# Four recurrent layers on one core: two sets of semaphores in turn, cleared by the next stage

## What is computed

```python
xn = _layernorm(x); s = _L0_attn_ref(xn, ...); g = _silu(_L0_ffn_ref(xn, ...)); x = x + s * g
xn = _layernorm(x); s = _L1_attn_ref(xn, ...); g = _silu(_L1_ffn_ref(xn, ...)); x = x + s * g
xn = _layernorm(x); s = _L2_attn_ref(xn, ...); g = _silu(_L2_ffn_ref(xn, ...)); x = x + s * g
xn = _layernorm(x); s = _L3_attn_ref(xn, ...); g = _silu(_L3_ffn_ref(xn, ...)); x = x + s * g
```

## Time and profile before

| | |
|---|---|
| three runs | 4060.0, 4065.36, 4072.39 us; median 4065.36 |
| the profiled execution: its time | 4061.12 us |
| its span in the trace | 4059.4 us |
| its mean granted TensorE clock | 0.967 of full speed |
| busy over the span | PE 85%, DVE 63%, ACT 44%, POOL 24% |
| DMA engines, mean over the span | 34 GB/s |

### The profile page before, as it was taken

The page is one execution under the profiler, slowest core; times in us unless marked ns, Lnnn a source line. Parts: engine busy times, 40 slices in busy tenths (PEclk is TensorE's granted clock), DMA queues, the critical chain, the costliest instruction groups (busy, mean ns, idle before and its releaser), DMA issues. The chain is left out here.

```text
span 4059.4 us, 56138 instructions
## 1 busy us (share of the span) xinstructions
PE 3448.3 (85%) x19803; PEld 1796.0 (44%) x19959; DVE 2564.1 (63%) x5512; ACT 1772.8 (44%) x3776; POOL 971.1 (24%) x809
## 2 busy tenths in 40 slices
PE   4888888888988889888988889888898888888877
PEld 2344434444344443444444443454434444444444
DVE  4566665666566665676556665666656766566665
ACT  1544434443444435444344444444354443444424
POOL 1032311332023320233113320233202231133234
PEclk7999999999999999999999999999999999999988
DMA  5000011101001020000110010110200101000130
GB/s 159 31 13 27 30 39 32 30 9 63 5 32 37 1 67 22 22 27 30 39 32 23 16 59 9 32 37 1 67 14 23 33 27 41 32 15 23 52 94 22
DMA packets 86675, 138.68 MB, mean 34 GB/s; under 512 B 12270, under 2 KB 61240, under 8 KB 83960
## 3 DMA queue, kind: packets, MB, share of 16 engines
q1 hardware_dynamic: 79636, 124.11, 9.6%
q10 hardware_dynamic: 6756, 10.87, 0.9%
HBM read 105.06 MB, written 29.10 MB: 33 GB/s over the span
## 5 line engine op out<-in xcount | busy, mean ns | idle before, releaser
L633 DVE TENSOR_REDUCE nmax<-banks 128x1 f32<-128x512 f32 (+3 forms) x1216 | 760.6, 658 | 415.5 <-PE banks L446 223.5
L556 ACT ACTIVATE probs<-banks 128x512 f32<-128x512 f32 (+3 forms) x1024 | 475.2, 526 | 291.6 <-PE banks L465 203.6
L446 PE MATMUL banks<-ks,qs 72*128 72x512 bf16 (+3 forms) x1536 | 442.4, 333 | 100.3 <-DVE nmax L633 60.5
L465 PE MATMUL banks<-qs,ks 74*128 74x512 bf16 (+3 forms) x1536 | 445.5, 331 | 47.7 <-ACT probs L556 19.7
L97 PE MATMUL banks<-filler,identb 128*128 128x512 bf16 x1632 | 425.0, 389 | 27.1 <-PEq L77 19.6
L446 PEld LDWEIGHTS banks<-ks,qs 72*128 72x128 bf16 x1536 | 141.4, 98 | 385.5 <-DVE nmax L633 214.8
L97 PEld LDWEIGHTS banks<-filler,identb 128*128 128x128 bf16 x1776 | 172.6, 100 | 222.8 <-issue 79.6
L556 ACT ACTIVATE early<-banks 128x256 f32<-128x256 f32 (+3 forms) x512 | 194.7, 440 | 169.7 <-PE banks L465 167.7
L1493 ACT ACTIVATE probs<-banks,nm 128x192 f32<-128x192 f32 x512 | 172.6, 422 | 214.0 <-DVE nm L1445 214.0
L515 PE MATMUL banks<-probs,v 128*32 128x512 f32 (+3 forms) x2048 | 234.4, 529 | 21.7 <-DVE att L620 10.3
L1527 POOL TENSOR_TENSOR probs<-probs,inv 128x768 f32<-128x768 f32 x128 | 187.2, 1467 | 253.8 <-DVE inv L1455 253.8
(11 more groups left out here) (490 smaller groups left out, 6661.9 us busy)
## 6 DMA issues: line engine op xcount, KB each, us to landing
qs<-parts_scratch SPq DMA_DIRECT2D x300, 96.0 KB
ks<-parts_scratch SPq DMA_DIRECT2D x288, 96.0 KB
parts_scratch<-parts SPq DMA_DIRECT2D x50, 384.0 KB, 2.5
shared<-in_w_h SPq DMA_DIRECT2D x17, 1024.0 KB, 7.6
shared<-in_w SPq DMA_DIRECT2D x26, 256.0 KB, 4.0
qs<-max_parts SPq DMA_DIRECT2D x192, 4.0 KB
xn<-in_x SPq DMA_DIRECT2D x9, 256.0 KB, 2.8
factor_scratch<-g SPq DMA_DIRECT2D x8, 256.0 KB, 2.3
```

Source lines behind the costliest of these rows:

```text
L446: mm = nc.tensor.matmul(K.ps[:, b, i * keys:(i + 1) * keys], K.qs[0:72, 4 * g + j, t * P:(t + 1) * P], K.ks[0:72, 4 * g + j, 0:keys], star ...
L465: mm = nc.tensor.matmul(K.ps[:, b, q0:T], K.ks[0:KR, h, k * P:(k + 1) * P], K.qs[0:KR, h, q0:T], start=True, stop=not on_tensor)
L556: nc.scalar.activation(probs[:, 4 * (q % QUADS) + m % 4, q0:T], K.ps[:, bank("second", m), q0:T], ACT.Exp, scale=scale).then_inc(exped, 1)
L633: nc.vector.tensor_reduce(nmax[:, t, h:h + len(heads)], K.ps[:, n % 2, 0:len(heads) * keys].rearrange("p (j k) -> p j k", k=keys), AX.X, A ...
```

## The change

There are now two pools, of 58 and 72 semaphores. `K.pool` is the one of the present stage, and `K.next_stage()` changes over while the program is built. Each stage clears the other pool on SP with `clear_last`; there is nothing behind a stage's own barrier. The semaphores of the row transfers (`saved`, `spread`) come in three sets, used in turn. The indices of some semaphores are lower, so that they fit.

```diff
-POOL = 85
+POOLS, EXPERTS = (58, 72), 24
...
-    def clear(self, spread=False, factor=True):
-        first = self.pool[0].num
-        self.nc.vector.sem_clear(range(first, first + (POOL + NG + 1 + factor if spread else POOL)))
-        self.nc.all_engine_barrier()
+    @property
+    def pool(self):
+        return self.pools[self.stage]
+    def next_stage(self):
+        self.stage = 1 - self.stage
+    def use_rows(self, i):
+        self.saved, self.spread = self.rows[i][0], self.rows[i][1:]
+    def clear_last(self, engine, rows=None, factor=False):
+        cleared = [self.pools[1 - self.stage]]
+        if rows is not None:
+            cleared.append(self.rows[rows])
+        if factor:
+            cleared.append([self.factor_stored])
+        for sems in cleared:
...
+            engine.sem_clear(range(sems[0].num, sems[0].num + len(sems)))
...
@@ prepare, SP @@
+                K.clear_last(sp, rows=layer - 1)
                 if save:
...
@@ attention, SP @@
                 if after_store:
+                    K.clear_last(sp)
                     sp.wait_ge(K.late_landed, 16 * K.late_loads)
+                elif fetched:
+                    K.clear_last(sp)
...
@@ local_attention, SP @@
+                if L == 0:
+                    K.clear_last(sp, factor=True)
                     spread_loads(nc, K, sp)
+                else:
+                    K.clear_last(sp, rows=2)
...
```

In the setup, the late loads move to POOL's queue, the ones of ks to VectorE, the mask casts ahead of the projections' work, and the quantisation is cut into steps:

```diff
@@ SP @@
                 fetch(sp, soon[0::2], soon_in)
-                fetch(sp, late[0:16], K.late_landed)
...
                 spread_loads(nc, K, sp, keys=False)
-                fetch(sp, late[28::2], K.late_landed)
@@ ACT @@
-                fetch(act, late[16:28], K.late_landed)
...
-                fetch(act, late[29::2], K.late_landed)
@@ POOL @@
-                nc.gpsimd.memset(K.ks[64:96, :, :], 1.0).then_inc(ones_set, 1)
-                pool.wait_ge(ones_set, 1)
                 nc.gpsimd.memset(K.filler[:, :], 1.0)
                 nc.gpsimd.memset(K.xnT[:, :], 0.0)
                 nc.gpsimd.memset(K.pb[:, :, :], 0.0)
                 nc.gpsimd.memset(K.y_experts[:, :, :], 0.0)
+                pool.wait_ge(gates_in, 16 * len(gates))
+                fetch(pool, late, K.late_landed)
@@ DVE @@
                 ch = Chain(dve, vec)
+                nc.vector.memset(K.ks[64:96, :, :], 1.0).then_inc(ones_set, 1)
                 for pad in pads:
...
-                nxt.run(nxt.on_vector)
+                nxt.run(nxt.on_vector, nxt.THIRD[1])
                 dve.wait_ge(first_in, 16 * len(first))
-                quantize_weights(nc, K, w4, q4, scr, ch, quantized)
+                steps = quantize_weights(nc, K, w4, q4, scr, ch, quantized)
+                for gate in nxt.GATED:
+                    next(steps)
+                    nxt.run(nxt.on_vector, gate)
+                for _ in steps:
+                    pass
```

In the final stage, the constants are loaded after the first two of the eight loads of `aet`, the step numbers of `late(n)` ahead of the chunks are lower (on ACT 6 to 17 become 3 to 13), VectorE's scans have more of the experts' work between them, and the experts' end is done in other parts. ACT computes a sigmoid in chunk 0 in place of the Silu, and POOL makes two products in chunk 1:

```diff
-        nc.scalar.activation(K.y_experts[:, :, :], K.y_experts[:, :, :], ACT.Silu).then_inc(self.y_done, 1)
+        nc.scalar.activation(self.sigmoid, K.y_experts[:, :, :], ACT.Sigmoid).then_inc(self.y_done, 1)
...
-        nc.gpsimd.tensor_tensor(self.factor, K.g[:, :, :], K.y_experts[:, :, :], ALU.mult).then_inc(self.f_ready, 1)
+        nc.gpsimd.tensor_tensor(K.g[:, :, :], K.g[:, :, :], K.y_experts[:, :, :], ALU.mult).then_inc(self.y_done, 1)
+        pool.wait_ge(self.y_done, 2)
+        nc.gpsimd.tensor_tensor(self.factor, K.g[:, :, :], self.sigmoid, ALU.mult).then_inc(self.f_ready, 1)
```

More of the change, by code:

```diff
@@ L60, in __init__, with many @@
         self.nc = nc
-        self.pool = [ctx.enter_context(nc.semaphore(f"sig{i}")) for i in range(POOL)]
-        self.saved = ctx.enter_context(nc.semaphore("parts_saved"))
-        self.spread = [ctx.enter_context(nc.semaphore(f"quad_spread{g}")) for g in range(NG)]
+        def many(name, n):
+            return [ctx.enter_context(nc.semaphore(f"{name}{i}")) for i in range(n)]
+        self.pools = [many("even", POOLS[0]), many("odd", POOLS[1])]
+        self.rows = [many(f"rows{i}_", 1 + NG) for i in range(3)]
         self.factor_stored = ctx.enter_context(nc.semaphore("factor_stored"))
         self.late_landed = ctx.enter_context(nc.semaphore("late_landed"))
-        first = self.pool[0].num
-        assert [s.num for s in self.pool + [self.saved] + self.spread + [self.factor_stored]] == list(
-            range(first, first + POOL + NG + 2))
-    def clear(self, spread=False, factor=True):
-        first = self.pool[0].num
-        self.nc.vector.sem_clear(range(first, first + (POOL + NG + 1 + factor if spread else POOL)))
-        self.nc.all_engine_barrier()
+        self.stage = 1
+        self.use_rows(0)
+    @property
[12 more added lines that the diff above has]
+        for sems in cleared:
+            assert [s.num for s in sems] == list(range(sems[0].num, sems[0].num + len(sems)))
+            engine.sem_clear(range(sems[0].num, sems[0].num + len(sems)))
 NAMED = {}
@@ L134, in quantize_weights @@
     values = w[:, :, :].rearrange("p c d -> p (c d)")
-    for _ in fp4_blocks(nc, ch, values, q[:, :, :].rearrange("p c d -> p (c d)"), *scr, P, 9 * D):
-        pass
+    yield from fp4_blocks(nc, ch, values, q[:, :, :].rearrange("p c d -> p (c d)"), *scr, P, 9 * D)
     nc.vector.engine_nop().then_inc(quantized, 1)
@@ L655, in _ @@
                     nc.vector.tensor_tensor(K.x[:, :, :], (x_in or K.x)[:, :, :], K.att[:, :, :], ALU.add)
-        K.clear(spread=True)
+        K.next_stage()
 class TernaryFfn(Beside):
@@ L973, in __init__ @@
         self.late = range(E3 - len(self.DOWN), E3)
+        self.sigmoid = K.xnT[:, :].rearrange("p (t d) -> p t d", t=NT)
     def scalar(self, act):
@@ L1531, in _ @@
                     next_power(nc, K, pool)
-        K.clear()
+        K.next_stage()
 class Glu(Beside):
@@ L2763, in _ @@
                     tokens(dst_, turned, use, n)
-            late(17)
+            late(13)
             nc.scalar.activation(sg_r[:, 0:4], K.ident[:, 0:4], ACT.Sigmoid).then_inc(warmed, 1)
@@ L2816, in _ @@
                 nc.scalar.activation(hp_sq[:, 1, :], dzp[:, 1, :], ACT.Square).then_inc(p_squared, 1)
+                if c == 0:
+                    late(17)
                 if c:
@@ L2893, in turn @@
                 mm.then_inc(done, 1)
-            late(6)
+            late(3)
             pe.wait_ge(mean_in, 16)
@@ L2898, in _ @@
                 means(j)
-                late(7 + j)
+                late(4 + j)
             shared_means(0)
-            late(11)
+            late(8)
             shared_means(1)
-            late(12)
+            late(9)
             pe.wait_ge(laid_out, 2)
@@ L2907, in _ @@
                     turn(src, use, n, turned)
-            late(13)
             pe.wait_ge(sp_act, 4)
@@ L3105, in _ @@
                         nc.gpsimd.tensor_tensor(share[:, :, :], q_f[:, :, :], coefficient[:, :, :], ALU.mult).then_inc(qab_done, 1)
+                if c == 1:
+                    work.run(work.on_gpsimd)
                 for t, g in units(c):
@@ L3167, in shares @@
                 dve.wait_ge(ab_ready, 2)
-            late(4)
+            late(2)
             first_weights()
-            late(6)
+            late(3)
             for j in range(J):
                 decay(j)
-                late(7 + j)
+                late(4 + j)
             shared_decay(0)
+            late(8)
             dve.wait_ge(et_ready, J)
@@ L3192, in _ @@
                                               t[:, :, :].rearrange("p j (c t) -> p j c t", t=CH)[:, :, :, CH - 1]))
-            late(14)
+            late(15)
             dve.wait_ge(k_squared, 2)
```

62 lines of the change are left out of this document (34 added, 28 removed).

## The result

The changed kernel takes **3967.7 us** (median of four runs, 3962.5 to 3971.9) against 4064.3 before: 0.9763 of the time, interval 0.9750 to 0.9775, so 96.5 us less. The forecast was 3994 with a range of 3975 to 4022.

What follows compares the result with a forecast made beforehand. TensorE was busy 87% of the loop; no engine bounded setup. Boundaries -59.4, setup -10.7 and final stage +0.7 sum to -69.4: 3991.7 from the profiled 4061.1, 3996.0 from the median, so 3994, range 3975 to 4022.

Steps and rivals of the forecast that it cites:

- The boundaries: At 66 stage ends, dropping the clear and second barrier saves 0.9 us each, 59.4 us in all.
- SP's clears: Eleven range clears per iteration on SP, at most 0.56 us each, all hidden in SP's waits: cost 0.
- Setup: POOL issues all 46 late loads at 1.04 us each from 9.1; setup ends at 57.3, not 68.0, saving 10.7 us.
- the cheap rival: In setup POOL issues at 0.56 to 0.84 us a load, VectorE's 47.4 ends it; total about 3984, chance 0.22.
- The four normalising operations: VectorE's operations in setup, 7.70 us beside POOL's memset, would take 1.4 without it.
- the chain's end: In setup, VectorE's memset, statistics and normalising would end near 13.0 instead of 14.2, a gain of some 1 us.
- the 47.4: Time in us at which VectorE would end its setup work; it decides the setup's end only if POOL is cheap.
- The rival of a starved POOL: VectorE's work in setup starves POOL's load issue, 2.9 us a load; setup ends at 143, total 4077, chance 0.03.
- Final stage: The edits behind the loop cost 0.7 us in sum, bounds -2 and +3.
- the products: In the final stage's chunk 1, POOL's two gate products of 1.26 us hold VectorE up by 1.9 us.
- The gain of 0.9 from the table load: In the final stage, the sigmoid's table load of 1.28 us goes mostly off the path, saving 0.9.
- Clock: Loop iterations vary by some 7 us with no edit; 10 us allowed to either side, no shift of the middle.

Runs made afterwards that it cites:

- the sets alone: Only the change's two sets of semaphores, setup and final stage as in the kernel before: 3997.0 us, ratio 0.9844 to the kernel before.
- the setup alone: The kernel before with only the change's setup, its clears and second barriers kept: 4064.8 us, ratio 1.0024.
- old_final_stage: The changed kernel with its final stage as it was before, loop and setup as changed: 3962.9 us, ratio 0.9746.
- The runs with barriers: The changed kernel with 3, 6 or 10 bare barriers behind the experts stage of each iteration: 4008.9, 4013.5 and 4020.6 us.
- 8 us of barriers: The changed kernel with 3 bare barriers behind the experts stage of each iteration: 4008.9 us, ratio 0.9871.

## Why the prediction was right and wrong

**The boundaries** were right: 59.5 us against 59.4, and each next stage starts at once.

**SP's clears** cost 0, as said. Their price was bounded by 0.56 and is 0.03 to 0.15 us on SP. I had counted eleven in an iteration; the trace's 96 are twelve. Doubling them cost nothing.

**Setup:** 57.6 us against 57.3, and only the sum was right. POOL's loads cost 0.55 each, the cheap rival's price, and not 1.04: whatever had slowed SP's last ones, POOL showed none of it. Those were also misread. Between 44.05 and 67.56 the trace has nine loads on SP, 2.61 each, and not eleven at 2.14; the mean would have been 1.10 and the setup's end 60.1. POOL's loads began at 14.6 and not at 9.1, since POOL runs in the program's order and its power (at 11.8) came after VectorE's memset. That memset began at 2.59 and not at 0.9. The four normalising operations took 1.30, as forecast, and the chain's end moved by 0, from 14.2 to 14.2. VectorE ended at 48.7, near the 47.4. What I left out is what decides: with POOL's loads under way SP waited 14.3 us for the stores of the parts (2.6 when POOL held back 28 of them), and the spread loads come behind. I had written that the spread loads on SP "are through when the last eleven late ones begin at 44.05, so neither decides", a time of a trace in which fewer transfers were queued ahead of them. The rival of a starved POOL did not appear. The Trainium skill, "SBUF — State Buffer", section "A bandwidth-pool intuition that's wrong (but worth ruling out)", has 0.62 us for one such transfer alone and 3.1 beside a VectorE copy. The trace has 0.55 a load and no sign of it, but it hardly tests the rule: of VectorE's 19.7 us beside the loads some 3 are casts and scalar operations.

**Final stage:** +4.0 in the profiled pair, +3 at equal clock, against +0.7 with a bound of +3. The loop was entered 0.24 earlier (0.3 said), and the products held VectorE up by 2.1 (1.9 said). The gain of 0.9 from the table load did not show. The rest of the +4.0 is not accounted for one by one; the stage also had 3 us more at the lower clock.

**Clock:** this is the step that failed. I wrote that an iteration varies by some 7 us with no edit, worked out that "eight at 473 would take 3784 instead of 3808", which is 24 less, and then wrote "I allow 10 us to either side", with the middle at zero. The runs showed that the loop's blocks took 32.7 us less with 79 us less at the lower clock. At equal clock the change gives 4053 - 3983 = 70 us, against the forecast's 69.4; the other 26 are the mean clock, 0.967 before and 0.976 after. That 70 meets 69.4 so closely is luck, since the slope errs by up to 10; the traces alone have 59.5 + 10.4 - 2.7 = 67 for the three terms.

It was no luck of a single run: the changed kernel had 0.973 to 0.978 in eight executions, the kernel before 0.962 to 0.972 in 50. But neither part alone brings that clock: the sets alone have 0.966 and the setup alone 0.962, while both together with the old final stage (`old_final_stage`) have 0.976. So it is not the 7.2 us per iteration by themselves. (The kernel before had 0.968 beside the first two and 0.965 beside the third; the changed kernel itself was not measured beside the first two.) The runs with barriers show that one more microsecond in each iteration is enough to lose that clock, and the run of the sets alone that another stretch ahead of the same loop is enough too. Which timing gives which clock stays open. With hindsight, the same middle of 3994 wanted a range of 30 us to either side, since another timing could as well have had a bad clock: 4009 at 8 us of barriers is 35 more than its own sum.

## What to carry to other kernels

When the same instructions repeat in a loop, a change in the length of an iteration, or only in what runs ahead of the loop, can shift the mean clock, by as much as 35 us of 4000 here: compare parts at equal clock, or stage by stage where the clock is 1.00, before a small edit is called good or bad. A clear that every engine must wait for costs a barrier more than itself (0.9 us against 0.56 here); put into the next stage, on an engine that waits anyway, it cost nothing. Loads moved to another queue are not out of the way: ask what is stored and read back while they are under way, and whether the drain at the block's end will wait for them.

## What the runs showed of the hardware that was not expected

- The range clear takes 558 ns on VectorE (85 semaphores or more) and 119 to 153 ns on SP for 58 or 72 semaphores, 30 to 45 for one or five.
- A bare barrier of all engines takes 0.33 us (21.2 us for 65).
- POOL's drain at the end of a block ended 1.9 us after the last of its loads had landed (48.5 to 50.4, 79.5 to 81.4); SP's took 0.3 us with its loads under way.
- POOL issued its loads at 0.55 us each with the transfer engines at 0.7 to 1.0 of their time busy, where SP's last nine had taken 2.6 at a mean of 0.75, one of them 9.6.
- Four kernels had 3.9 to 4.4 us outside their span in every execution, and the others 1.7 to 2.2. It is not explained.
- The same loop code, with nothing added, mostly had iterations of 464 us with 10 us at the lower clock in the changed kernel, and in the kernel with the sets alone, behind another setup, iterations of 465.5 to 471 with 17 to 31.
